# Three cross-attentions: the output product at the end of its step, its addition one step later

## What is computed

```python
q = (xq @ q_w).reshape(B, N, H, D)
attn = softmax(einsum('bnhd,bmhd->bhnm', q, k) * scale)   # x1: masked first
out = einsum('bhnm,bmhd->bnhd', attn, v).reshape(B, N, C)
x = x + (out @ proj_w + proj_b)
```

## Time and profile before

| what | before |
|---|---|
| timed runs, us | 997.67, 1002.45, 1002.10 (median 1002.1) |
| the profiled execution, us | 999.13 (its span 997.2) |
| mean granted clock of TensorE | 0.947 of full speed |
| busy share of the span | PE 86%, DVE 74%, ACT 63%, POOL 55% |
| the chain that ended last, by engine | PE 51%, DVE 24%, ACT 14%, issue 5% |
| x1 alone, from its first G to its fifth | 407.9 to 445.2 us |
| x2, from its first G to its fourth | 514.9 to 539.3 us |
| ca, from its first G to its sixth | 749.0 to 788.6 us |
| moe | from about 797 us to the end |

### The profile page before, as it was taken

One profiled execution on the slowest core, in us unless ns is written; L12 is line 12 of the kernel. 1 busy time (PEld: TensorE's weight loads), 2 busy tenths in 40 slices (PEclk: granted clock), 3 DMA queues, 4 the chain that ended last, 5 costly groups with the idle time before them and its releaser, 6 DMA issues.

```text
span 997.2 us, 23673 instructions
## 1 busy us (share of the span) xinstructions
PE 857.8 (86%) x8603; PEld 520.7 (52%) x8603; DVE 736.9 (74%) x1592; ACT 626.9 (63%) x1551; POOL 552.6 (55%) x1069
## 2 busy tenths in 40 slices
PE   5988888865657779998999899999988789999996
PEld 2444444433334445555755456555555557676765
DVE  5788898778884655666567667667557787999986
ACT  1899999958883214544355455554556477686875
POOL 2688888866652335763345565556344254647533
PEclk9999999877876889999999899999999999999998
DMA  8500000000000000000000010000000000000000
GB/s 257 179 2 2 0 0 2 1 1 1 1 1 1 1 0 1 2 2 1 1 2 2 20 25 24 24 24 20 1 2 2 1 2 1 2 7 7 7 7 22
DMA packets 23579, 16.48 MB, mean 17 GB/s; under 512 B 8744, under 2 KB 20400, under 8 KB 23344
## 3 DMA queue, kind: packets, MB, share of 16 engines
q1 hardware_dynamic: 23472, 15.06, 5.3%
HBM read 10.85 MB, written 1.05 MB: 12 GB/s over the span
## 4 chain that ended last, share of the span: by engine, by line
PE 51%; DVE 24%; ACT 14%; issue 5%; POOL 3%; SPq 2%; DMA 1%; DVEq 0%; ACTq 0%; POOLq 0%
ACT sb_E L1276 10%; PE ps_context L799 5%; PE ps_context L802 3%; PE ps_scores L875 3%; PE ps_scores L899 2%; DVE sb_inv_den L1816 2%; PE ps_turned L1176 2%; PE ps_turned L1114 2%; PE ps_scores L792 2%; PE ps_scores L752 2%; PE ps_turned L1178 2%; PE ps_turned L1177 2%; DVE sb_neg_half L1784 2%; PE ps_turned L713 2%; PE ps_scores L1155 2%
## 5 line engine op out<-in xcount | busy, mean ns | idle before, releaser
L1276 ACT ACTIVATE sb_E<-ps_scores,sb_neg_max,sb_score_scale 128x256 f32<-128x256 f32 (+1 forms) x384 | 190.9, 515 | 20.8 <-DVE sb_neg_max L1577 15.0
L2335 POOL TENSOR_SCALAR sb_E<-sb_E,sb_inv_sum 128x256 f16<-128x256 f32 x256 | 123.6, 483 | 27.1 <-DVE sb_inv_sum L1613 7.3
L1529 ACT ACTIVATE sb_E<-ps_scores,sb_ff_bias 128x512 f32<-128x512 f32 x128 | 88.2, 691 | 45.3 <-PE ps_scores L1155 41.7
L1784 DVE TENSOR_REDUCE sb_neg_half<-ps_scores 128x16 f32<-128x1024 f32 x48 | 58.7, 1222 | 67.1 <-PE ps_scores L875 67.1
L1596 DVE TENSOR_REDUCE sb_neg_quad<-ps_scores 128x2 f32<-128x512 f32 (+1 forms) x96 | 64.3, 684 | 43.0 <-PE ps_scores L754 30.9
L713 PE MATMUL ps_turned<-sb_ident 128*128 128x512 f16 x289 | 86.7, 421 | 9.4 <-DVE sb_ident_b L2200 9.4
L1304 ACT ACTIVATE sb_E<-ps_scores 128x512 f32<-128x512 f32 x96 | 57.0, 598 | 46.5 <-PE ps_scores L794 45.3
L2268 POOL TENSOR_SCALAR sb_veps<-sb_mv 128x2 f32<-128x2 f32 x72 | 19.9, 276 | 119.1 <-DVE sb_mv L1554 118.1
L1572 DVE TENSOR_REDUCE sb_neg_raw<-ps_scores 128x4 f32<-128x1024 f32 x64 | 77.8, 1216 | 7.6 <-PE ps_scores L685 7.6
L1401 ACT ACTIVATE sb_E<-ps_scores 128x1024 f32<-128x1024 f32 x48 | 49.1, 1023 | 54.6 <-PE ps_scores L907 54.5
L1276 ACT ACTIVATION_READ_ACCUMULATOR sb_E<-ps_scores,sb_neg_max,sb_score_scale 128x1 f32 x384 | 79.9, 208 | 0.0
(11 more groups left out here) (302 smaller groups left out, 2588.2 us busy)
## 6 DMA issues: line engine op xcount, KB each, us to landing
sb_moe_up<-in_moe_up SPq DMA_DIRECT2D x1, 2048.0 KB
sb_KS<-sb_qk_parts SPq DMA_DIRECT2D x96, 16.0 KB, 1.8
sb_QS<-sb_qk_parts SPq DMA_DIRECT2D x96, 16.0 KB, 1.8
sb_rows<-in_rows SPq DMA_DIRECT2D x1, 1216.0 KB, 7.7
out_x<-sb_raw_context SPq DMA_DIRECT2D x8, 128.0 KB, 1.8
sb_X<-in_x SPq DMA_DIRECT2D x1, 768.0 KB, 10.1
sb_square<-in_square SPq DMA_DIRECT2D x1, 768.0 KB, 11.3
sb_ctxT<-in_ctxT SPq DMA_DIRECT2D x1, 512.0 KB, 11.4
```

The costliest lines, as they stand in the source:

```text
L1276: last = act.activation(E[:, ring, head], SC[t % 2][:, head], ACT.Exp, bias=neg_max[:, ring, h:h + 1], scale=scale, accum_out=row_sum[:, r ...
L1529: last = act.activation(U_full[:, n % RING, :], banks[n % 4], ACT.Gelu, bias=bias, scale=1 / WEIGHT_SCALE)
L1784: dve.tensor_reduce(neg_half[:, n % 2, :, :, :].rearrange("p x i g -> p (x i g)"), SC[0][:, :].rearrange("p (h k) -> p h k", k=CTX), AX.X, ...
L2335: last = pool.tensor_scalar(E16[:, ring, SEQ * h:SEQ * h + SEQ], E[:, ring, SEQ * h:SEQ * h + SEQ], inv_sum[:, ring, h:h + 1], HALF, ALU.m ...
```

## The change

The round G goes from the head of the even step, behind its scores, to its very end, behind T. The addition to x goes from the even step, behind its maximum, to the odd step after it, also behind its maximum and ahead of the reciprocal; in the last step (20), which no odd one follows, it stays. `rounds_of` lists the rounds in the new order, so the banks are dealt out anew: in the steady part Q takes the bank of the T before it, T that of the G of the step before, and G that of the Q of its own step.

```diff
@@ CrossAttention.rounds_of
-        return [("G", m - 3), ("Q", m + 1), ("T", m + 2)] if step % 2 == 0 else []
+        return [("Q", m + 1), ("T", m + 2), ("G", m - 3)] if step % 2 == 0 else []
@@ TensorE, cross_step
                 half_scores(L, B, n)
                 if n % 2 == 0:
-                    cross_round(L, B, "G", m - 3)
                     cross_round(L, B, "Q", m + 1)
...
                 half_keys(L, B, n - 1)
                 if n % 2 == 0:
                     cross_round(L, B, "T", m + 2)
+                    cross_round(L, B, "G", m - 3)
@@ VectorE, cross_step
                 half_max(L, B, n)
                 if n % 2 == 0:
-                    add_to_x(L, B, m - 3)
                     queries_lo(L, B, m + 1)
                     cross_stats(L, B, m + 3)
                 elif n >= 5:
+                    add_to_x(L, B, m - 3)
                     cross_context(L, B, (n - 5) // 2)
+                if n == L.LAST:
+                    add_to_x(L, B, m - 3)
```

## The result

| | before | after |
|---|---|---|
| median of the timed runs (4 each) | 1002.28 us | 988.62 us |
| lowest, highest | 997.67, 1003.79 | 983.42, 990.95 |
| profiled execution, its span | 999.13, 997.2 | 987.16, 985.3 |
| TensorE busy in the span | 857.8 (86%) | 858.5 (87%) |
| mean granted clock | 0.947 | 0.943 |

The ratio of the times is 0.9865, 95% interval 0.9829 to 0.9901: 13.7 us less by the medians, 12.0 between the two profiled executions. Forecast were 991 us and 11.2 us.

What follows compares the result with a forecast made beforehand. TensorE alone bounds x1; in x2 and ca it waits for G's late input. Gains of 12.6 less 1.4 for gaps give 11.2 us, from the 1002.10 median 990.9, taken as 991; forecast 988 to 994, range 985 to 998.

Steps and rivals of the forecast that it cites:

- step 2: At G's new place between T and the odd scores: gaps of 0 to 0.21 in 14 batches, 1.4 us lost.
- Step 1: G leaves the even step's head in x1, x2, ca: waits over 0.21 return 11.25 us, 12.6 with hidden G.
- The third case: Without G's wait, the values or odd scores wait instead; 1000 to 1002 us, chance 0.09.
- The ends: Ends of x1 and ca: G of step 16 hides in the values' wait for exponentials, 0.41 to 0.55 us each.
- Step 3: VectorE's round through G's wait for L1796: 7.22 us against TensorE's 7.24, so G waits nothing or some 0.1.
- the rival with a chance of 0.18: VectorE's round becomes the bound in x2 and ca, or gaps reach their upper end; 994 to 998 us, chance 0.18.
- The seam: From x2 to sa: QK takes the bank of batch 3's G with 0.3 us left, costed at nothing; G hides in T's stall.
- the rival with full clock at the seam: At sa's start the clock drop is shorter or absent, worth up to 3.4 us; 985 to 989 us, chance 0.08.
- One sign that I had named: In the changed trace, half clock showing in new places would make the prediction wrong; no size given.
- The slower rival: G blocks the odd scores in x2 and ca, from 1.0 us beyond 7.22; 1006 us at 8.7, chance 0.03.
- The clock: Short idles between matmuls make no clock swing, since ca with waits of about 1 us stayed at 1.00; no term.

Runs made afterwards that it cites:

- four copies: Changed kernel with four copies of the denominators added ahead of each reciprocal of the cross-attentions on VectorE; 1004.61 us.
- the kernel before with 1.44 of idle a pair: Kernel before the change with two copies of the denominators added ahead of each reciprocal of the cross-attentions; 1021.51 us.

## Why the prediction was right, point by point

The forecast was 991.0, faster, by 11.2 us; measured were 988.6, and 13.4 us in the stretches that the change can touch. Term by term (the forecast with 0.1 a batch for the gaps of step 2):

| stretch | gain forecast | gain measured |
|---|---|---|
| x1, rounds | -0.2 | 0.24 |
| x1, end | 0.93 + 0.47 | 1.92 |
| x2, rounds | 3.80 - 0.4 | 3.74 |
| x2's end and seam | 0.47 | 0.25 |
| ca, rounds | 4.86 - 0.5 | 4.60 |
| ca, end | 1.34 + 0.47 | 2.68 |
| sum | 11.2 | 13.4 |

The timed median of 988.6 lies near the lower end of the forecast's 988 to 994. All lines but the seam's gave more than their term, so the sum was too small by 2.2 us for the reasons that follow.

**Step 1, the waits given back.** Right in mechanism and size. A wait less 0.21 was forecast for each; a ca pair shortened by 8.18 - 7.15 = 1.03 for 1.04, the ends by 0.91 for 0.93 and 1.33 for 1.34 (by the run with the cheap reciprocal in the old order). The 0.21 stayed: it is now ahead of L944's load. The third case, that the wait comes back elsewhere, did not come: TensorE is busy for the whole of the three stretches.

**The ends, mis-sized.** The sum gave the new order 0.47 at each end, for a G that hides in a later wait. Measured are 1.01 and 1.35. What was left out is what G was moved past a second time: at steps 17 and 18 it stood ahead of the last values, and ScalarE's copy of the last context waited for these. In ca's end, before and then after:

```profile
793.97 0.61 PE L961 MATMUL ps_turned<-sb_square,sb_context 128*128 128x128 f32 x4
794.51 0.64 PE L799 MATMUL ps_context<-sb_E,sb_VCTX 128*32 128x256 f32 x8
795.65 0.60 ACT L1409 ACTIVATE sb_raw_context<-ps_context 128x512 f32<-128x512 f32 x1 [3.23 <-PE ps_context L802]
796.30 0.97 PEld L1185 LDWEIGHTS ps_context<-sb_router_w,sb_hT 128*128 128x128 f32 x8 [1.20 <-ACT sb_raw_context L1409]
```

```profile
782.57 0.64 PE L799 MATMUL ps_context<-sb_E,sb_VCTX 128*32 128x256 f32 x8
783.57 0.71 PE L961 MATMUL ps_turned<-sb_square,sb_context 128*128 128x128 f32 x4
783.70 0.60 ACT L1409 ACTIVATE sb_raw_context<-ps_context 128x512 f32<-128x512 f32 x1 [2.78 <-PE ps_context L802]
784.36 0.97 PEld L1185 LDWEIGHTS ps_context<-sb_router_w,sb_hT 128*128 128x128 f32 x8 [0.27 <-ACT sb_raw_context L1409]
```

Before, G at 793.97 held the values, the copy and the router's product (L1185) up; now it runs beside the copy, and the idle ahead of L1185's load falls from 1.20 to 0.27. From L1083, which stands ahead of all of these (at 793.48 and 781.98), to L1185 it was 2.82 and is 2.38: 0.44 that I had put on no path. x1's end has the same shape, with the table load of L1501 behind the copy, and the same 0.44 (L1083 to L1114). The order makes it, not the wait: with the copy in the old order L1083 to L1185 is still 2.82, with the copy in the new one 2.38. A further 0.24 of ca's end are values that waited for the exponentials behind a late G (0.45 ahead of their load, at 785.22) and now show 0.21 at most. 0.1 in x1 and 0.2 in ca aren't accounted for. Nor did I size rightly what the addition of steps 17 holds back: behind it batch 6's reciprocal started 1.9 us after its input's copy (L1409) ended in x1 and 1.3 in ca, where I had said up to 1. It cost nothing, for the next G shows 0.41 of idle, as it does behind the values where it waits for nothing.

**Step 2, the gap at the new place.** Taken as 0.1 for each of 14 batches, bounds 0 and 0.21. It has two values, not one: 0 where T stands ahead (nine batches) and 0.21 behind the keys (steps 12 and 14). G's load in steps 12 and 14 of ca starts at 767.5 and 773.97 with 0.21 of idle. The lower bound was the truth for the rounds that repeat, and that is most of the rest of the difference in x2 and x1.

**Step 3, VectorE's round.** The circle is the right one: G waits for L1796 as soon as it is longer, by just the excess (7.31 and 8.24 worked out, 7.29 and 8.22 measured). Its length was over-stated: 7.22 forecast, 7.15 - 0.27 = 6.88 measured. From the rows above: 0.96 + 1.14 + 0.33 + 1.78 + 0.35 + 1.13 + 0.47 + 0.06 + 0.65 = 6.87. The addition counts its pitch of 0.33, not its duration of 0.41; the step to TensorE is 0.06, not 0.2 (the two times that I gave for it, 761.57 and 761.70, are 0.13 apart, and they lie on the way to VectorE); and the product's pitch is 0.35, not 0.57. G to scores is 0.65 for 0.55 and TensorE's own round 7.15 for 7.24. So the rival with a chance of 0.18 was 0.27 us a pair away, not 0.02.

The product is where the rule of the Trainium skill, "SBUF — State Buffer", section "Who interferes with whom", did better than my sum, which left it out. In ca GpSimd's L2287 ran from 757.57 to 758.29 and the product started at 758.26 with 0.42 us; with the addition elsewhere it is 0.65. By that rule I had given 7.0. I had shortened it, though: the section leaves out of its exemption for a single SBUF input the instructions in a 2-port mode, and it names copies among those that can enter one. The trace agrees with it, for a copy took 0.81 us beside GpSimd and 0.28 alone.

**The seam.** QK and the addition cost nothing visible. Of the 0.47 for the hidden G 0.25 shows, in a stretch of 177 us that varied by several us between the profiles. The stall is 2.15 (about 2.3 forecast) and the half clock behind it is still there, 0.51 over 7 us: the rival with full clock at the seam was wrong. One sign that I had named does show, half clock in a new place: 3.4 us at 569.5, where the kernel before has none but has one at 697.8. The kernel changed in ca alone, whose x2 and seam are the old ones, has the like at 576.0, so it is no mark of the change.

**The slower rival** had the right circle and the right turning point, but needed 1.0 us beyond the forecast round, 1.3 by the measured one. With four copies (1.36 more) a pair of ca is at 8.22, as long as before the change.

**The clock.** I gave the short idles between matmuls no term, since ca stood at 1.00 with 1.25 us of idle a pair. For this change that holds: both kernels are at 1.00 in the rounds of ca. But the kernel before with 1.44 of idle a pair fell to half speed within ca. So the 1.00 of one kernel did not show that such idles stay harmless when they grow a little. The Trainium skill, "TensorE: Matmul & The Clock Gate", section "A second HAM failure mode: psum-queue depth-cycling", warns of that swing, and this run agrees with it, where the kernel before did not show it. It is one execution, and what in it brought the clock down the runs don't settle.

## What to carry to other kernels

A product whose input comes a little late belongs behind the other work of its step in the engine's queue, not at its head; what to check is the circle that it then closes through the bank it writes, by pitches and not by durations. A few added copies test its slack: the pairs came out within 0.02 us of what it foretold. Where a step is moved, follow also what stood behind it on other engines' queues at the ends of the loops: there, the move gave as much again as the wait it removed. And compare two traces between fixed points: two executions of the same code differed by up to 6 us before the change began.

## What the runs showed of the hardware that was not expected

- A step from VectorE to TensorE through a semaphore has two sizes here, from the end of the one to the weight load of the other: 0.05 to 0.06 us where G waited for L1797 (766.68 to 766.73), 0.12 where it waited for the product (765.26 to 765.38). What makes the difference is open.
- The idle ahead of G's load where nothing holds it up depends on what stands ahead of it: none behind T's f32 transposes, 0.21 behind the keys or the even scores, 0.41 behind the values. It isn't T alone: the scores' load behind T shows 0.17 with G between the values and the keys.
- A VectorE copy of 128x256 f32 between SBUF tiles takes 0.28 alone, at a pitch of 0.20 to 0.23 behind another, and 0.65 to 1.24 beside a GpSimd instruction.
- In the one execution with 1.44 us of idle in pairs of 8.37 the clock fell to half speed (1.2 GHz) twice in the rounds of x2 and twice in those of ca, 3.4 us each; with 1.25 in 8.18 the rounds of ca stayed at full speed.
